# A state-space scan whose products are put in order of the TensorE tiling

## The reference, cut to what matters

```python
def step(state, inp):
    x_t, b_t, c_t, dt_t = inp
    decay = jnp.exp(dt_t * a)[..., None, None]
    b_bar = dt_t[..., None] * b_t
    state = decay * state + b_bar[..., None] * x_t[:, :, None, :]
    y_t = jnp.einsum('bhn,bhnp->bhp', c_t, state)
    return (state, y_t)
...
y = _ssd_scan(xh, b, c, dt, a)
y = y + d_param[None, None, :, None] * xh
mean = yg.mean(axis=(1, 3), keepdims=True)
var = yg.var(axis=(1, 3), keepdims=True)
```

## Time and profile before

| | before |
|---|---|
| median of three runs | 1427.3 us |
| the profiled execution | 1426.3 us, its span 1424.2 us |
| mean granted TensorE clock | 0.989 |
| TensorE busy | 1361.9 us (96%) |
| VectorE busy | 966.0 us (68%) |
| ScalarE busy | 686.9 us (48%) |
| GpSimd busy | 287.5 us (20%) |
| chain that ended last, by engine | PE 84%, DVE 8%, issue 4%, ACT 2% |

### The profile page before, as it was taken

The page is one execution under the profiler, slowest core; times in us unless marked ns, Lnnn a source line. Parts: engine busy times, 40 slices in busy tenths (PEclk is TensorE's granted clock), DMA queues, the critical chain, the costliest instruction groups (busy, mean ns, idle before and its releaser), DMA issues.

```text
span 1424.2 us, 24617 instructions
## 1 busy us (share of the span) xinstructions
PE 1361.9 (96%) x9379; PEld 826.1 (58%) x9379; DVE 966.0 (68%) x2777; ACT 686.9 (48%) x1351; POOL 287.5 (20%) x388
## 2 busy tenths in 40 slices
PE   7999999999999999999999999999999997999984
PEld 3446645676457665576456764576655763566543
DVE  2425797487874787567974878747875679747682
ACT  4534643645445562646436454455626454363312
POOL 3004201241104201042012411042010420133110
PEclk9999999999999999999999999999999998999997
DMA  7100001020000200020010200002000200101010
GB/s 276 42 0 31 16 16 48 1 79 30 26 23 6 75 30 26 23 80 16 15 49 1 79 30 26 23 8 73 30 26 23 80 16 15 49 3 49 30 48 5
DMA packets 47556, 54.32 MB, mean 38 GB/s; under 512 B 7624, under 2 KB 42312, under 8 KB 47440
## 3 DMA queue, kind: packets, MB, share of 16 engines
q1 hardware_dynamic: 41424, 46.41, 9.6%
q0 software_dynamic: 6016, 6.35, 1.7%
HBM read 34.84 MB, written 17.85 MB: 37 GB/s over the span
## 4 chain that ended last, share of the span: by engine, by line
PE 84%; DVE 8%; issue 4%; ACT 2%; POOL 1%; DMA 1%; POOLq 0%; SPq 0%; DVEq 0%
PE ps L1564 42%; PE ps L1743 8%; PE ps L1687 5%; PE ps L1643 4%; DVE yst L1169 3%; PE ps L1702 2%; PE ps L1655 2%; PE ps L1883 2%; PE ps L1893 2%; PE ps L1634 2%; PE ps L1661 1%; PE ps L1671 1%; PE ps L1848 1%; PE ps L1814 1%; PE ps L1676 1%
## 5 line engine op out<-in xcount | busy, mean ns | idle before, releaser
L1564 PE MATMUL ps<-xT,wb_s 128*128 128x512 f32 x512 | 233.2, 602 | 3.6 <-ACT xT L730 3.5
L1564 PE MATMUL ps<-xT,wc_s 128*128 128x512 f32 x512 | 225.4, 593 | 0.0
L1564 PEld LDWEIGHTS ps<-xT,wc_s 128*128 128x128 f32 x512 | 96.1, 190 | 112.3 <-issue 111.9
L1564 PEld LDWEIGHTS ps<-xT,wb_s 128*128 128x128 f32 x512 | 94.2, 191 | 113.3 <-issue 104.7
L1055 DVE SCALAR_TENSOR_TENSOR xT<-xc,cols_s,xT 128x512 f32<-128x512 f32 x192 | 134.9, 749 | 2.7
L1564 PE MATMUL ps<-hT,wx_s 128*128 128x512 f32 x256 | 117.7, 603 | 3.2 <-ACT hT L688 2.8
L1564 PE MATMUL ps<-hT,wz_s 128*128 128x512 f32 x256 | 112.8, 593 | 0.1
L1743 PE MATMUL ps<-CT,xT 128*128 128x256 f32 x512 | 111.9, 379 | 0.9 <-DVE xT L1227 0.9
L755 ACT ACTIVATE BT<-ps 128x512 f32<-128x512 f32 x64 | 37.9, 592 | 150.8 <-PE ps L1564 150.8
L1743 PEld LDWEIGHTS ps<-CT,xT 128*128 128x128 f32 x512 | 97.2, 190 | 17.8 <-issue 5.0
L755 ACT ACTIVATE CT<-ps 128x512 f32<-128x512 f32 x64 | 38.1, 595 | 125.3 <-PE ps L1564 125.3
(11 more groups left out here) (297 smaller groups left out, 2456.0 us busy)
## 6 DMA issues: line engine op xcount, KB each, us to landing
xr<-x SPq DMA_DIRECT2D x8, 1024.0 KB, 9.2
x_scratch<-xr SPq DMA_DIRECT2D x32, 256.0 KB, 2.1
out<-EC SPq DMA_DIRECT2D x32, 256.0 KB, 2.1
BT<-x SPq DMA_DIRECT2D x7, 1024.0 KB, 5.7
modrow<-mod_scratch SPq DMA_DIRECT2D x8, 512.0 KB, 6.7
w_s<-w SPq DMA_DIRECT2D x2, 1024.0 KB, 11.0
BT<-x SPq DMA_DIRECT2D x2, 512.0 KB, 6.0
xT<-wmod SPq DMA_DIRECT2D x1, 1024.0 KB, 11.1
```

The lines of the kernel that those rows point to most:

```text
L1564: ins = t_.matmul(bank[:, :], w[:, k, m * P:(m + 1) * P], rhs[:, k, half * HALF:(half + 1) * HALF], start=k == 0, stop=k == nk - 1)
```

## The change

TensorE's loop over the chunks becomes turn(c+1), cumdiff(c+1), scores(c+1), inter(c), intra(c), state(c). The products of cumdiff and of scores are cut in two along their output rows, so that both run in 64x64 tiles: cumdiff's 2 products become 4 and scores' 8 become 16, with as many streamed columns in each as before. `output` is split into `inter` and `intra`. On VectorE `masked(c+1)` moves ahead of `state(c)`, and with it the pieces of the next batch's norm and the first `y_stats`, which stood behind `masked`; the pieces are also shared out otherwise (tiles 0 and 1 in chunk 3; 2, 3 and the first variance in chunk 4; 4 to 7 and the second variance in chunk 5). VectorE's `state` waits for y no more, and its `skip` now waits for the state's product too; TensorE's `state` no longer waits for `y_ready`.

```diff
@@ VectorE, scan
                     dve.wait_ge(s_filled, at(s_filled, b, c + 1))
                     if c:
                         dve.wait_ge(Sdc_ready, at(Sdc_ready, b, c))
-                    dve.wait_ge(y_filled, at(y_filled, b, c + 1))
...
                 def skip(c):
 
                     dve.wait_ge(y_filled, at(y_filled, b, c + 1))
+                    if c < T - 1:
+                        dve.wait_ge(s_filled, at(s_filled, b, c + 1))
...
                     if c + 1 < T:
                         weigh(c + 1)
+                        masked(c + 1)
+
+                    if c == 3 and not last:
+                        mod_column(b + 1)
+                        ln_stats(b + 1, (0, 1))
+                    if c == 4 and not last:
+                        ln_stats(b + 1, (2, 3))
+                        ln_var(b + 1, 0)
+                    if c == 5 and not last:
+                        ln_stats(b + 1, (4, 5, 6, 7))
+                        ln_var(b + 1, 1)
+                        chA.end()
+                    if c == 6:
+                        y_stats(0, 0, 4)
                     if c < T - 1:
                         state(c)
                     else:
                         y_stats(1, 4, 7)
                     skip(c)
-                    if c + 1 < T:
-                        masked(c + 1)
-
-                    if c == 3 and not last:
-                        mod_column(b + 1)
-                        ln_stats(b + 1, (0, 1, 2, 3))
-                        ln_var(b + 1, 0)
...
@@ TensorE, cumdiff
-                        t_.matmul(ps[s][:, :], Lw[r, c * P:(c + 1) * P], R8[r, :, c * P:(c + 1) * P],
-                                  start=True, stop=False)
+                        for d in (slice(0, 64), slice(64, 128)):
+                            t_.matmul(ps[s][d, :], Lw[r, c * P + d.start:c * P + d.stop],
+                                      R8[r, :, c * P:(c + 1) * P], start=True, stop=False)
...
@@ TensorE, scores
-                            ins = t_.matmul(ps[2 + s][:, k * P:(k + 1) * P], BT[r, c // 4, k, chunk(c)],
-                                            CT[r, c // 4, k, chunk(c)], start=True, stop=True)
+                            r, o = slice(64 * s, 64 * s + 64), chunk(c).start
+                            for d in (slice(0, 64), slice(64, 128)):
+                                ins = t_.matmul(ps[2 + s][d, k * P:(k + 1) * P],
+                                                BT[r, c // 4, k, o + d.start:o + d.stop],
+                                                CT[r, c // 4, k, chunk(c)], start=True, stop=True)
...
@@ TensorE, scan
                 for c in range(T - 1):
                     turn(c + 1)
                     cumdiff(c + 1)
-                    state(c)
-                    output(b, c)
+                    scores(c + 1)
+                    inter(b, c)
                     if c == T - 2 and not last:
                         ln_in(b + 1, 0)
-                    scores(c + 1)
+                    intra(b, c)
+                    state(c)
```

More of the change, by code:

```diff
@@ L1620, in carry_rows, with inter @@
                               start=True, stop=True).then_inc(proj.filled[q % 4], 1)
-            def output(b, c):
+            def inter(b, c):
                 if c or later(b):
@@ L1636, in output, with intra @@
                                       skip_group_check=k >= 2)
+            def intra(b, c):
                 pe.wait_ge(Xd_ready, at(Xd_ready, b, c + 1))
@@ L1685, in scores @@
                         for s in range(2):
-                            r = slice(64 * s, 64 * s + 64)
-                            ins = t_.matmul(ps[2 + s][:, k * P:(k + 1) * P], BT[r, c // 4, k, chunk(c)],
-                                            CT[r, c // 4, k, chunk(c)], start=True, stop=True)
+                            r, o = slice(64 * s, 64 * s + 64), chunk(c).start
[3 more added lines that the diff above has]
+                                                CT[r, c // 4, k, chunk(c)], start=True, stop=True)
                             if k == KC - 1:
@@ L1696, in state @@
                         pe.wait_ge(S_ready, at(S_ready, b, c))
-                        pe.wait_ge(y_ready, at(y_ready, b, c))
                     for k in range(KC):
@@ L1901, in batch @@
                 if f is not None:
-                    output(f, T - 1)
+                    inter(f, T - 1)
+                    intra(f, T - 1)
                 x_proj(b, 0, (1,))
```

## The result

The changed kernel takes 1402.45 us in the median (four runs, 1400.85 to 1405.66) against 1427.52: a ratio of 0.9825, 95% interval 0.9806 to 0.9844. It is 25 us faster; 29 were predicted, and 1402.45 lies inside the range of 1387 to 1410, though 0.45 above the forecast's own stretch of 1393 to 1402. The profiled execution took 1402.87, its span 1400.7, at a mean granted clock of 0.988.

What follows compares the result with a forecast made beforehand. TensorE was taken to set the scan's pace, its turn falling from 4.91 to 4.24 us. Seven batches save 3.55 each (24.9), the last 3.8, in sum 28.7, giving 1398 us after rounding; range 1387 to 1410.

Steps and rivals of the forecast that it cites:

- the forecast's own stretch: Whole kernel: a time of 1393 to 1402 us, given a chance of 0.57.
- The bound and the price of a tiling: Scan turn: TensorE sets the pace; handing over to another tiling costs 0.09 to 0.11 us, entering 0.04 to 0.09.
- Quarters four abreast: Scores and differences in 64x64 tiles: four run side by side, scores 0.87 us (bounds 0.87 to 1.74), differences 0.22.
- The rival by which column halves take turns: Scores and differences: column halves of one row half queue, turn 5.32 us against 4.91, total about 1443; chance 0.07.
- The rival by which the change of operands is what costs: Scan turn: every change of operand costs, not tiling; turns gain only 0.07 us, total 1424; chance 0.04.
- VectorE's cover: Chunks 1 to 3: VectorE's 3.32 us of pieces fit into a 4.24 turn, 0.6 to 0.8 to spare.
- The new wait at inter(6): TensorE in turn 6: inter(6) waits 1.5 us for VectorE's skip, behind the norm's pieces, in each of seven batches.
- x lands in time: Chunk 3: the next batch's x lands 5.7 us behind its issue, about 0.2 after VectorE gets there, and is hidden.
- rival 2: Scan: entries left (0.19 a turn) or VectorE waits in chunks 3 and 4; about 9 us lost, 1407; chance 0.18.
- The last batch: Batch without norm pieces: keeps only the 3.8 us of turns 0 to 5 and its start; `gn_stats` reached at 14.3.

Runs made afterwards that it cites:

- the two experiments: Changed kernel with differences and scores back in halves, 1419.51 us; kernel before with only differences and scores cut into quarters, 1420.67 us.
- the filled kernel: Changed kernel with x loaded by two DMAs, ln_in ahead of inter(6) and the first statistics split around state(6) and skip(6): 1393.91 us, again 1394.71.

## Why the prediction was right, and where it was off

- **The bound and the price of a tiling.** Right. Handing over costs 0.09 to 0.11 and entering 0.04 to 0.09: the causal group fell from 0.23 to 0.11, scores from 1.09 to 0.87, and putting the halves back brought 1.09 back. That adjoining groups pay nothing was taken from chunk 0 alone and held for a step from bfloat16 to float32 too. Turn 0, though, came out at 3.97 and not 3.80: its scores start only as VectorE's masked(0) is done, and cost 1.04 there.
- **Quarters four abreast.** Right at the lower bound, 0.87. The rival by which column halves take turns (1443 us) is refuted by 32 rows in 0.87. With it falls what the prediction drew from the Trainium skill, "TensorE: Matmul & The Clock Gate", Part 3, by which a weight load overlaps running products only when its row group differs: column halves of one row half do run side by side here. The rival by which the change of operands is what costs (1424) is refuted by the turn of 4.27, with the same eight groups as before, and by the two experiments, whose gains go by the count of tiling changes.
- **VectorE's cover.** Right: chunks 1 to 3 wait for nothing, and masked ahead of the state is needed (5.78 a turn without).
- **The new wait at inter(6).** Right in place and cause, 1.1 to 1.4 instead of 1.5. VectorE's pieces overlap their successors: masked costs 1.2 to the next start, not 1.26, and weigh 0.6, not 0.69.
- **x lands in time.** The step that failed. "That is hidden" went by the median of 5.7. The kernel before asked for x 6.5 us behind the issue in every batch, and its latest part landed at 5.8. The changed kernel asks at about 5.5. In three of its seven batches the last of 16 parts landed at 6.8 to 7.1. There VectorE waits in chunk 3, and TensorE 0.5 to 0.9 us at inter(4). These three batches are 3.0 us longer in sum than the undisturbed second batch, the two with a stall for instructions 1.6, which the prediction had no term for: 4.6 together. This is the half of rival 2 that speaks of VectorE's waits in chunks 3 and 4 (1407); its other half, entries left inside the blocks, is refuted by the scores' 0.87. In the eight profiles in which x is one DMA, 56 loads in all, the last part landed either by 5.84 or from 6.42 to 7.26. The 17 late ones all have a 16 KB packet of the same instruction queue that starts within 5.3 us of their issue. Of the 39 others 13 have one too, and the kernel before has only one such load in seven. That the packet is the cause is not shown by an experiment: moving the other loads left the late landings.
- **The last batch.** The prediction kept 3.8; measured is 45.8 to 44.2, so 1.6. Its chain was right (inter(7) waits 3.33 for the skip), but it reached `gn_stats` 15.75 into turn 6 and not 14.3, and was compared with the wrong batch: before, the last batch got there at 13.8, 0.6 sooner than a middle one. The prediction had no term for the clock either. Behind the wait the granted clock is 0.5 (1.2 GHz) from 1287.6 to 1291.0, and intra and the three projections take 7.9 us where the filled kernel's second profile, with the full clock there, has 6.3.

```profile
1286.61 0.67 PE L1633 MATMUL ps<-EC,Sst 64*64 64x128 f32 x16 [3.33 <-DVE xT L1164]
1287.21 1.61 PE L1643 MATMUL ps<-Mt,XB 128*64 128x128 f32 x16
...
1288.75 6.54 PE L1564 MATMUL ps<-hT,wz_s 128*128 128x512 f32 x12
...
1295.12 0.28 PE L1735 MATMUL ps<-pk,halfmean 128*128 128x8 f32 x2
```

These windows of the changed kernel, of the filled kernel and of its second run cover what follows that wait; the granted clock is the third column from the end.

```profile
1286.00:1291.00 5.00, 4.39 (x35) 2.81 (x36) 4.49 (x15) 0.00 (x0) 0.00 (x0) 0.66 0.01 3
```

```profile
1277.00:1286.00 9.00, 8.38 (x44) 4.32 (x45) 6.67 (x25) 1.20 (x2) 0.35 (x1) 0.81 0.01 2
```

```profile
1276.00:1284.00 8.00, 7.06 (x47) 3.85 (x47) 6.99 (x26) 1.19 (x2) 0.65 (x1) 1.00 0.01 2
```

The last two are one program, with a wait of 2.01 at inter(7) in both: where the clock fell it reached `gn_stats` 14.44 into turn 6, where it did not, 12.79. So the fall costs about 1.6 us. It is there in all six profiles in which inter(7) waits over 3 us, and not in the kernel before. VectorE's pk is ready over 3 us ahead there: the first statistics ahead of state(6) hold this batch up. With them behind skip(6) its inter(7) waits 1.56 and the batch takes 41.4 at full clock instead of 44.2. Three projections stand behind the wait and could stand in it; that wasn't tried.

The two misses, 4.6 and 2.2, make 6.8. Against them stand 1.1 that was gained between the scans (119.6 to 119.5 in each batch, 0.5 in the first) and 0.6 ahead of the first scan and behind the last, neither of them predicted; the spans differ by 23.5, predicted 28.7. That a middle batch gained 3.52 where 3.55 was predicted is partly luck: up to the start of turn 6 it gained 3.2 and not 3.8, and from there to `gn_stats` it gained 0.3 where a loss of 0.3 was predicted.

## What to carry to other kernels

Count the changes of tiling in a loop of small products before you count the products. A change cost 0.15 to 0.17 us here, about one and a half of the MATMULs of 128 columns (0.109) in the full array, and cutting a product into smaller tiles is free where four then run abreast, and pays once its neighbours have the same tiling. When such a gain makes one engine faster, look at each load that was just in time by its latest part, not by the median, and at the work that the other engine has ahead of what it must deliver. The best kernel here, 1389.16 us, took the same two steps further: the wait filled with work that was ready, and bulk loads moved away from the scan's densest stretch of instructions. And when an engine waits longer than it did, price the clock too: here a wait of 3.3 us brought 1.6 more behind it.

## What the runs showed that I had not expected

- TensorE seems to run out of instructions in a dense stretch: 0.1 to 2.3 us, in two to four batches of each of the eight profiles that have it, always with an instruction packet that starts while a load of 1 MB is under way, and not once in the two profiles in which those loads were issued 12 us later.
- Between single executions of the same kernel the stretch behind the last `gn_stats` differed by 3 us (105.6 and 109.0 in the changed kernel's two profiles). These two windows of those profiles, start to end of the stretch, show the granted clock in the third column from the end: 0.90 and 0.86.

```profile
1295.00:1400.00 105.00, 76.65 (x431) 47.95 (x435) 62.81 (x197) 29.27 (x72) 13.36 (x16) 0.90 0.09 28
```

```profile
1298.00:1406.00 108.00, 79.39 (x431) 50.77 (x435) 62.84 (x197) 29.28 (x72) 13.39 (x16) 0.86 0.09 27
```

  TensorE falls from 2.4 to 1.2 GHz for some of the last stage, where it waits for other engines, and not for the same time in each execution. Over all thirteen profiles the stretch takes 105.6 to 106.3 us in nine and 107.95 to 109.0 in four, and these four are the ones in which one of the falls of the clock there, other than the last, lasts 10.2 or 13.7 us; in the nine none of these lasts over 3.4. That alone is 0.2% of the whole, as much as a small change here would give.
